# Turning the rows for the router with VectorE and a round trip through memory, in a cross-attention + mixture-of-experts kernel

## The chip, the cores and the metric

The kernel runs on one core of one Trainium2 chip. The metric is the device time of one execution in microseconds (us), lower is better; before the change the median of three runs is 1381.79 us (1377.54 to 1382.42).

## The reference, cut to what matters

8192 tokens (4 sequences of 2048) of width 512 go through two layers, all in float32:

```
x1  = layernorm(x)
q,k,v from x1 (512x512) and ctx (77 x 384); 16 heads of 32; softmax(q k / sqrt(32)) v
x2  = x + relu(attn @ W1 + b1) @ W2 + b2            # 512 -> 1024 -> 512
z   = layernorm(x2)
top1 = argmax(z @ Wg.T)                             # 8 experts, first of equal maxima
out = x2 + [gelu((layernorm(z)*s_e + b_e) @ w1_e + b1_e) @ w2_e + b2_e](top1)
```

Each token goes to one expert only. The router needs `x2` with its 512 features on the partitions (transposed), because TensorE contracts over partitions; the expert stage needs the normalised rows of `x2`, sorted by expert.

## The kernel before, in words

Tokens are worked in 16 blocks (`b` = 0 to 15) of 512, each in 4 subtiles (`SUB`) of 128 rows. Most products are done as three fp32r products of high and low parts (`split3`). One list, `sched`, written out by hand (lines 264 to 576), gives the order of all steps; `walk` then has every engine, SyncE (SP) and GpSimd (POOL) among them, issue its own part of each step in that order. Every engine's instructions run in the order of the list, so a wait in one step holds up all later steps of that engine. A bank of PSUM is chosen for each step that needs one: the one that was left longest ago.

One turn of the loop over `b` (line 364) is:

1. The last head group (`g` = 3) of the attention of block `b`: SUMS, RC (DVE reciprocal), AV, NORM, OUT. Between them TT: 16 PE transposes of the rows of `x2` of the previous block (`pe_tt`), evicted by ACT to `x2T` (TTOUT).
2. The up-projection: tiles `m` = 0 to 7 of 12 matmuls each (H on PE, two ACT passes HHI, one DVE pass HLO). The first two tiles are worked group by group (HK 0 to 3), as the attention output comes in; HK 3 is the last to become ready.
3. Woven into it: L (logits, 32 small matmuls), LT (transposed back), OH (one-hot of the maximum, DVE), RK (ranks, 8 small matmuls and six DVE operations), and SCAT (four indirect DMAs by POOL that scatter the normalised rows of block `b`-1 to `region`). When the scatters have landed, XLOAD (SP) loads the raw rows of block `b`+1 over them.
4. Also in it, on DVE: XSTAT for block `b`+1, a chain of 28 steps (statistics of `xn`, inverse root, normalising, four 32x32 block transposes into `xq`), dealt out by DRIP and finished by DRAIN at `m` = 4; and X2STAT, the chain that scales the rows of block `b`-1.
5. XTD: 16 DMAs by SP from `xq` back into `xn`, which complete the transposition of `x`; XTS then splits the result into `actA` (ACT high part, DVE low part).
6. The down-projection of subtiles 0 and 1 (YA, Y; 24 matmuls each), then Q of block `b`+1 (four tiles of 12 matmuls), which needs all four XTS. The maxima (SM), scores (ST, named by their matmul line 1126) and the rest of the attention of block `b`+1 follow, with the down-projection of subtiles 2 and 3 in pieces between them (YP).

`xn` is loaded by XNLOAD (SP). For `b` outside 3 to 10 (and under 15) the step stands in turn `b` behind HK 3 and loads block `b`+1; its lines are

```
            elif not PREP0 < b <= PREP0 + NE:
                step("XNLOAD", b + 1, 2)
                step("XNLOAD", b + 1, 0)
```

In turns 2 to 9 one expert's weights are also prepared. There the second weight is loaded by SP (E2_RAW, behind XLOAD in the list) into part of `xn`, split by ACT (E2_HIGH, between the ACT passes of Q tiles 1 and 2) and DVE (E2_LOW), and XNLOAD of block `b`+2 follows. In turns 3 to 10 DVE also scales the first weight (E1_ACC, in the up-projection).

`xq` lies in the low half of `actQ`, `x2T` in its high half. After the loop the experts run over 71 tiles of sorted rows.

Of the kernel before, what the change touches and what calls it, by code (L numbers as in the profile page):

```python
# [27 lines left out]
P = 128  # L28
D = 512
# [33 lines left out]
PREP0 = 2  # L63
DT = 2


def xattn_moe_kernel(nc, A, out):
    region = nc.dram_tensor("region", [NE * REG + P, ROW], F32).ap()
    v_parts = nc.dram_tensor("v_parts", [NB - 1, M, D], F32).ap()
    e1_parts = nc.dram_tensor("e1_parts", [P, KD, NE, EH], F32).ap()  # L70
    e2_parts = nc.dram_tensor("e2_parts", [2, P, NE, D], F32).ap()

# [161 lines left out]
    with ExitStack() as ctx:  # L234
        bank = [ctx.enter_context(nc.psum_tensor(f"bank{i}", [P, 512], F32)) for i in range(8)]

        def sem(name):
# [3 lines left out]
        L = {n: sem(f"ld_{n}") for n in (  # L241
            "bk", "first", "consts", "wk", "wv", "ctx", "wq", "w1", "w2", "e1", "e2", "eb", "jt", "tab", "pad0", "e1raw", "e2raw", "eb1")}
        ld_xn = [sem(f"ld_xn{s}") for s in range(SUB)]
        ld_x = [[sem(f"ld_x{i}_{s}") for s in range(SUB)] for i in range(2)]
        ld_xT = [sem(f"ld_xT{t}") for t in range(SUB)]
        st_v, ld_v = sem("st_v"), sem("ld_v")
# [7 lines left out]
            "dve_bks pe_k act_kf act_k dve_k pe_v dve_v pool_zero dve_const "  # L254
            "act_wq dve_wq act_w1 pool_w1 act_w2 dve_w2 act_kbd dve_sel dve_tri "
            "dve_xn dve_xnT pool_xb pe_xT act_xT dve_xT pe_q act_q dve_q pe_sm dve_max pe_mt act_mt pe_s act_exp "
            "pe_sums dve_rc pe_av dve_n act_o pool_o dve_o pe_h act_h dve_h pe_y dve_x2 dve_row pool_ones pe_gate dve_gate "
# [106 lines left out]
        for b in range(NBLK):  # L364
# [7 lines left out]
            if b:  # L372
                step("SUMS", b, g)
                step("RC", b, g)
                step("AV", b, g)
                for s in range(SUB - 1):
                    step("TT", b - 1, s)
                step("NORM", b, g)
                step("TTOUT", b - 1, 0)
# [27 lines left out]
            logits = 2  # L407
            ranks = 4 if last else 6
            for m in range(MF):
                if m >= 2:  # L410
                    step("H", b, m)
                step("HHI", b, m)
                if b and m == logits:
                    step("L", b - 1)
                    if last:
                        step("E2_LOAD", 0)
                if b and m == logits + 1:
                    step("LT", b - 1)
                if b and m == ranks:
# [10 lines left out]
                if b and m == logits + 1:  # L430
# [9 lines left out]
                if b and m == ranks:  # L440
                    for s in range(SUB):
                        step("SCAT", b - 1, s)
                    if not last:
                        step("XLOAD", b + 1)
# [32 lines left out]
            else:  # L477
# [85 lines left out]
        for t in range(-5, NT):  # L563
# [113 lines left out]
        def sp_setup(sp):  # L677

            sp.dma_start(bk[:], A["bk"]).then_inc(L["bk"], 16)
            sp.dma_start(ctxT[:], A["ctxT"]).then_inc(L["ctx"], 16)  # L680
            sp.dma_start(wk_raw[:], A["Wk"]).then_inc(L["wk"], 16)
# [102 lines left out]
        def sp_padload(sp):  # L784
            for s in range(SUB):
                sp.wait_ge(scat[0][s], 16 * (NBLK // 2))
            sp.dma_start(padrow[:], A["padrow"]).then_inc(L["tab"], 16)
            sp.dma_start(regions[:], A["regions"]).then_inc(L["tab"], 16)
            sp.wait_ge(L["tab"], 32)

            sp.dma_start(region[NE * REG:NE * REG + P, :], padrow[:]).then_inc(L["pad0"], 16)

# [32 lines left out]
        def dve_masks(dve):  # L825
            dve.wait_ge(L["consts"], 16 * NSMALL)
            dve.tensor_copy(tri[:], c_raw[:, 0:P])
            dve.tensor_copy(ones[:], c_raw[:, P:2 * P]).then_inc(S["dve_tri"], 1)

# [37 lines left out]
        def pe_kp(pe, m):  # L867
            p = own_bank(pe, "KP", m)
            if m == 0:
                pe.wait_ge(L["ctx"], 16)  # L870
                pe.wait_ge(L["wk"], 16)
            for k in range(KT):
# [99 lines left out]
        def dve_xstat(dve, b):  # L972

            def chain():
# [20 lines left out]
        def pe_xT(pe, b, s):  # L995
# [6 lines left out]
            mm.then_inc(S["pe_xT"], 1)  # L1002

        def sp_xtd(sp, b):

            sp.wait_ge(S["dve_xnT"], SUB * (b - DT + 1))
            for t in range(SUB):
                for f in range(HG):
                    sp.dma_start(xn[t][HD * f:HD * f + HD], xq[HD * t:HD * t + HD, f].rearrange("p k s j -> p (k s j)")
                                 ).then_inc(ld_xT[t], 16)  # L1010

# [192 lines left out]
        def pe_hk(pe, b, k):  # L1204

            if b == 0:
                pe.wait_ge(S["pool_w1"], 1)
# [4 lines left out]
            for m in range(2):  # L1212
                mm = h_products(pe, b, m, k)
# [69 lines left out]
        def dve_x2stat(dve, b):  # L1283


            def chain():
# [7 lines left out]
                for s in range(SUB):  # L1294
                    dve.wait_ge(S["pe_tt"], SUB * b + s + 1)
# [14 lines left out]
        def act_tt(act, b, s):  # L1310

            act.wait_ge(S["pe_tt"], SUB * b + s + 1)
            act.activation(x2T[b == NBLK - 1][:, :, P * s:P * s + P],
# [3 lines left out]
        def pe_l(pe, b):  # L1317

            p = own_bank(pe, "L", b)
            if b == 0:  # L1320
                pe.wait_ge(S["dve_const"], 1)
            pe.wait_ge(S["act_tt"], SUB * (b + 1))
            for k in range(KD):
                for s in range(SUB):
                    mm = pe.matmul(p[HD * s:HD * s + HD, 0:P], wg[:, k, :], x2T[b == NBLK - 1][:, k, P * s:P * s + P],  # L1325
                                   start=k == 0, stop=k == KD - 1)
# [274 lines left out]
        def sp_bload(sp, t):  # L1601
# [9 lines left out]
            if t == N1:  # L1611
                for s in range(SUB):
                    sp.wait_ge(scat[1][s], 16 * (NBLK // 2))
                sp.wait_ge(st_pad, 16 * NE)
                sp.wait_ge(L["pad0"], 16)
            if t >= NROW:
# [120 lines left out]
        def pool_store(pool, t):  # L1737
# [26 lines left out]
            "XT": {"pe": pe_xT, "act": act_xT, "dve": dve_xT},  # L1764
            "XTD": {"sp": sp_xtd},
            "XTS": {"act": act_xts, "dve": dve_xts},
# [21 lines left out]
            "Y": {"pe": pe_y, "dve": dve_y},  # L1788
            "X2STAT": {"dve": dve_x2stat},
            "TT": {"pe": pe_tt},  # L1790
            "TTOUT": {"act": act_tt},
# [125 lines left out]
```

## Time and profile before

| | |
|---|---|
| median of 3 runs | 1381.79 us |
| the profiled execution | 1382.66 us |
| its span | 1380.9 us |
| PE busy | 1358.1 us (98%) |
| DVE busy | 1000.4 us (72%) |
| ACT busy | 609.0 us (44%) |
| POOL busy | 338.0 us (24%) |
| mean granted TensorE clock | 0.999 |

The span is the stretch from the first to the last instruction in the trace; the execution's own time is 1.8 us longer. Busy time of PE is modelled from pipelined matmuls and so is no proof of work at the peak; the chain of waits says which engine the end is followed back to. An engine with 72% busy time may still be the one that is late in a short stretch.

### The profile page before, as it was taken

To read this page: it belongs to the slowest core of one execution; us is meant where nothing else is said; L and a number is where in the kernel's file an instruction comes from. 1 tells how busy PE (TensorE), PEld (TensorE's weight loads), DVE (VectorE), ACT (ScalarE), POOL (GpSimd) and SP (SyncE) were. 2 spreads that over 40 slices of the span, in tenths; PEclk is the share of its full clock that TensorE was granted. 3 is DMA by queue.
4 is the path that set the end of the run, shared out by engine and by line. 5 is a ranking of instruction groups with operands and counts; after the bars stand their busy time and mean duration, and the time that the engine had idled before them with its cause. 6 is when DMAs were issued, how large, how long until landed. Compare 5 with 4: busy or idle time off the path is not lost.

```text
span 1380.9 us, 23796 instructions
## 1 busy us (share of the span) xinstructions
PE 1358.1 (98%) x8366; PEld 1015.2 (74%) x8366; DVE 1000.4 (72%) x2129; ACT 609.0 (44%) x1146; POOL 338.0 (24%) x293
## 2 busy tenths in 40 slices
PE   7999999999999999999999999999999999999997
PEld 5486868677776768686868677776868686788996
DVE  6777677687778777777878677867676767558666
ACT  4434334443434343534344343524343433357885
POOL 2311211103020212121120202021212121128886
PEclk9999999999999999999999999999999999999999
DMA  7200302213040404131231303040303032559884
GB/s 297 76 29 3 93 31 67 88 36 123 22 139 9 138 24 117 50 101 61 63 99 31 123 25 114 6 122 1 117 7 106 18 92 76 189 170 302 285 260 140
DMA packets 66998, 132.85 MB, mean 96 GB/s; under 512 B 11241, under 2 KB 19698, under 8 KB 65986
## 3 DMA queue, kind: packets, MB, share of 16 engines
q1 hardware_dynamic: 56082, 97.63, 23.5%
q0 software_dynamic: 10800, 33.70, 6.4%
q8 instruction: 70, 1.15, 0.3%
q14 instruction: 46, 0.38, 0.1%
HBM read 73.77 MB, written 44.66 MB: 86 GB/s over the span
## 4 chain that ended last, share of the span: by engine, by line
PE 94%; DVE 2%; issue 1%; DMA 1%; POOL 1%; ACT 0%; another core or an unknown queue 0%; SPq 0%; POOLq 0%; ACTq 0%; DVEq 0%
PE bank L1221 25%; PE bank L1265 13%; PE bank L1245 12%; PE bank L1054 12%; PE bank L1144 8%; PE bank L1126 5%; PE bank L1647 4%; PE bank L1685 3%; PE bank L1079 2%; PE bank L1307 2%; PE bank L1631 2%; PE bank L1325 1%; PE bank L1098 1%; PE bank L898 1%; DMA region<-rows,pos 0%
## 5 line engine op out<-in xcount | busy, mean ns | idle before, releaser
L1221 PE MATMUL bank<-actA,w 128*128 128x512 f32 x1536 | 368.6, 395 | 1.4 <-DVE actA L1192 1.4
L1221 PEld LDWEIGHTS bank<-actA,w 128*128 128x128 f32 x1536 | 282.4, 188 | 63.4 <-issue 5.6
L1134 ACT ACTIVATE E<-bank 77x512 f32<-77x512 f32 x256 | 132.5, 592 | 172.8 <-PE bank L1126 172.7
L1265 PE MATMUL bank<-w,actH 128*128 128x512 f32 x768 | 195.7, 400 | 0.0
L1396 POOL DMA_INDIRECT region<-rows,pos x64 | 66.5, 1039 | 487.0 <-DVE rows L1296 451.6
L1054 PE MATMUL bank<-actA,wq 128*128 128x512 f32 x768 | 182.7, 390 | 0.0
L1245 PE MATMUL bank<-w,actH 128*128 128x512 f32 x768 | 179.6, 391 | 0.0
L1092 DVE TENSOR_REDUCE mx<-bank 128x4 f32<-128x308 f32 x256 | 104.8, 473 | 95.0 <-PE bank L1079 94.9
L1265 PEld LDWEIGHTS bank<-w,actH 128*128 128x128 f32 x768 | 138.7, 188 | 44.6 <-issue 18.3
L1245 PEld LDWEIGHTS bank<-w,actH 128*128 128x128 f32 x768 | 143.4, 188 | 29.5
L1054 PEld LDWEIGHTS bank<-actA,wq 128*128 128x128 f32 x768 | 142.7, 188 | 28.2 <-issue 0.5
L1230 ACT ACTIVATE actH<-bank,b 128x512 fp32r<-128x512 f32 x128 | 88.3, 690 | 159.3 <-PE bank L1221 157.7
L1235 DVE TENSOR_TENSOR actH<-bank,actH 128x512 fp32r<-128x512 f32 x128 | 87.6, 689 | 58.5 <-ACT bank L1231 56.5
L1161 DVE RECIPROCAL att<-bank 128x512 f32<-128x512 f32 x32 | 107.3, 3354 | 23.1 <-PE bank L1144 22.8
L1187 POOL TENSOR_TENSOR actA<-att,actA 128x512 fp32r<-128x512 f32 x32 | 41.0, 1281 | 331.7 <-ACT actA L1181 331.7
L1063 ACT ACTIVATE actQ<-bank,bq 128x512 fp32r<-128x512 f32 x64 | 43.9, 685 | 145.5 <-PE bank L1054 145.5
L1161 DVE RECIPROCAL csb<-bank 128x512 f32<-128x512 f32 x32 | 106.9, 3341 | 0.3 <-PE bank L1144 0.3
L1044 POOL TENSOR_TENSOR rows<-rows,b2bc 128x512 f32<-128x512 f32 x64 | 81.9, 1290 | 68.2 <-DMA rows<-in_x 43.3
L1231 ACT ACTIVATE bank<-bank,b 128x512 f32<-128x512 f32 x128 | 83.8, 655 | 0.0
L1275 DVE TENSOR_TENSOR rows<-bank,rows 128x512 f32<-128x512 f32 x64 | 44.2, 691 | 54.0 <-PE bank L1265 28.7
L1740 POOL DMA_INDIRECT out<-rowB x71 | 77.2, 1087 | 24.5 <-issue 11.8
L1647 PE MATMUL bank<-xhT,ew 128*128 128x128 f32 x568 | 75.9, 276 | 4.1 <-DVE gT L1674 2.3
(182 smaller groups left out, 1831.2 us busy)
## 6 DMA issues: line engine op xcount, KB each, us to landing
rowB<-region SPq DMA_DIRECT2D x71, 258.0 KB
xn<-in_x SPq DMA_DIRECT2D x64, 256.0 KB
rows<-in_x SPq DMA_DIRECT2D x64, 256.0 KB, 3.4
xn<-xq SPq DMA_DIRECT2D x224, 64.0 KB, 2.0
w_raw<-in_W SPq DMA_DIRECT2D x2, 2048.0 KB, 11.8
e_raw<-in_E SPq DMA_DIRECT2D x16, 256.0 KB, 3.4
region<-padrow SPq DMA_DIRECT2D x9, 258.0 KB, 2.3
e_parts<-e_high SPq DMA_DIRECT2D x8, 256.0 KB, 2.5
```

The source lines that it names most:

```text
L1054: mm = pe.matmul(p[:], w, a, start=k == 0 and j == 0, stop=k == KD - 1 and j == 2)
L1092: dve.tensor_reduce(to, p, AX, ALU.max, negate=True).then_inc(S["dve_max"], 1)
L1134: act.activation(E[0:M, g % 2, h, :], of("ST", b, g, h)[0:M, :], ACT.Exp).then_inc(S["act_exp"], 1)
L1144: mm = pe.matmul(p[r, :], held(h), E[0:M, g % 2, h, :], start=True, stop=True)
L1161: dve.reciprocal(att_of(g)[:], of("SUMS", b, g)[:]).then_inc(S["dve_rc"], 1)
L1221: mm = pe.matmul(p[:], w, a, start=k == 0 and j == 0, stop=k == KD - 1 and j == 2)
L1230: act.activation(actH[:, 0, m, :], p[:], ACT.Relu, bias=b1[:, m:m + 1])
L1231: act.activation(p[:], p[:], ACT.Relu, bias=b1[:, m:m + 1]).then_inc(S["act_h"], 1)
L1235: dve.tensor_tensor(actH[:, 1, m, :], of("H", b, m)[:], f32(actH[:, 0, m, :]), ALU.subtract).then_inc(S["dve_h"], 1)
L1245: mm = pe.matmul(p[:], a, w, start=m == 0 and j == 0, stop=m == MF - 1 and j == 2)
L1265: mm = pe.matmul(p[:], actH[:, ha, m, P * s:P * s + P], w2[:, hw, m, :], start=n == 0, stop=n == 23)
L1647: mm = pe.matmul(p, ew[t % 2][:, k, :], xhT[t % 2][:, k, :], start=k == 0, stop=k == KD - 1)
```

## The change

TT and TTOUT are left out for blocks 0 to 13 (`TP` = 14). In their place a step TTR turns the rows with four DVE block transposes into `xq`, one DMA stores `xq` to memory, SP waits for it to land, and four DMAs load it as `x2T`. XSTAT waits for the store before it writes `xq`. L, LT, OH, RK, SCAT and XLOAD move from the up-projection into the down-projection (in turns 1 to 14). Three tiles of the up-projection are worked by groups (`NHK` = 3). Four of the 16 DMAs of XTD go to POOL. DRIP deals nine steps in place of six.

```diff
+TP = NBLK - 2
+NHK = 3
+    x2_parts = nc.dram_tensor("x2_parts", [SUB, HD, HG, D], F32).ap()
@@ sched, turn b
                 step("AV", b, g)
-                for s in range(SUB - 1):
-                    step("TT", b - 1, s)
+                if last:
+                    for s in range(SUB - 1):
+                        step("TT", b - 1, s)
                 step("NORM", b, g)
...
                 step("OUT", b, g)
-                step("TTOUT", b - 1, 1)
-                step("TTOUT", b - 1, 2)
-            for m in range(2):
+                if last:
+                    step("TTOUT", b - 1, 1)
+                    step("TTOUT", b - 1, 2)
+                else:
+                    step("TTR", b - 1)
+            for m in range(NHK):
                 step("H", b, m)
             step("HK", b, 0)
             step("HK", b, 1)
             step("HK", b, 2)
-            if b:
+            if last:
                 step("TT", b - 1, SUB - 1)
                 step("TTOUT", b - 1, SUB - 1)
             step("HK", b, 3)
...
-                if b and m == logits:
+                if last and m == logits:
                     step("L", b - 1)
...
-                    step("DRIP", 6)
+                    step("DRIP", 6 if last or b == 0 else 9)
...
                 step("YA", b, 0)
-                for s in range(SUB):
-                    step("XB", b + 1, s)
+                if b:
+                    step("L", b - 1)
                 step("Y", b, 0)
+                if b:
+                    step("LT", b - 1)
+                    step("OH", b - 1)
                 for s in range(2):
                     step("XTS" if b + 1 >= DT else "XT", b + 1, s)
                 step("YA", b, 1)
+                if b:
+                    step("RK", b - 1)
+                    for s in range(SUB):
+                        step("SCAT", b - 1, s)
+                    step("XLOAD", b + 1)
+                for s in range(SUB):
+                    step("XB", b + 1, s)
@@ dve_xstat
                 if b >= DT:
-                    dve.wait_ge(S["pe_s"], KD * b)
+                    dve.wait_ge(st_x2, 16 * (b - 1))
@@ sp_xtd; pool_xtd issues the other four
+        NSP = 12
+                    if HG * t + f < NSP:
+                        sp.dma_start(*quarter(t, f)).then_inc(ld_xT[t], 16)
@@ new
+        def dve_ttr(dve, b):
+            dve.wait_ge(S["pe_s"], KD * (b + 2))
+            dve.wait_ge(S["dve_x2"], SUB * (b + 1))
+            for s in range(SUB):
+                dve.transpose(xq[:, :, :, s, :], rows[b % 2][:, s, 0:D].rearrange("p (k f j) -> p f k j", k=KD, j=HD)
+                              ).then_inc(S["dve_tq"], 1)
+
+        def sp_ttr(sp, b):
+            sp.wait_ge(S["dve_tq"], SUB * (b + 1))
+            if b:
+                sp.wait_ge(ld_x2T, 16 * SUB * b)
+            sp.dma_start(x2_parts.rearrange("t i f n -> (t i) (f n)"), xq[:].rearrange("p f k s j -> p (f k s j)")
+                         ).then_inc(st_x2, 16)
+            sp.wait_ge(st_x2, 16 * (b + 1))
+            sp.wait_ge(S["pe_s"], KD * (b + 2))
+            for t in range(SUB):
+                sp.dma_start(x2T[0][:, t, :], x2_parts[t].rearrange("i f n -> f i n")).then_inc(ld_x2T, 16)
@@ pe_l
-            pe.wait_ge(S["act_tt"], SUB * (b + 1))
+            if b < TP:
+                pe.wait_ge(ld_x2T, 16 * SUB * (b + 1))
+                x = x2T[0][:].rearrange("p t (k s j) -> p k s t j", k=KD, s=SUB)
```

The rest of the diff gathers a few semaphores of the set-up and adapts the waits to the new counts.

## Rows read from the trace of the kernel before

**Rows 1.** The page: busy time by engine; the chain's shares by engine.
```profile
PE 1358.1 (98%) x8366; PEld 1015.2 (74%) x8366; DVE 1000.4 (72%) x2129; ACT 609.0 (44%) x1146; POOL 338.0 (24%) x293
PE 94%; DVE 2%; issue 1%; DMA 1%; POOL 1%; ACT 0%; another core or an unknown queue 0%; SPq 0%; POOLq 0%; ACTq 0%; DVEq 0%
```
**Rows 2.** The chain of waits in turn 14: start us, us, what.
```profile
1097.58 1.46 PE bank L1307 x12
1099.04 4.13 PE bank L1221 x18
1103.18 0.44 PE bank L1307 x4
...
1107.75 1.01 PE bank L1325 x32
...
1133.93 5.44 PE bank L1054 x24
...
1148.12 1.09 PE bank L1126 x16
```
**Rows 3.** VectorE in order of time, turn 14: start us, us, instruction, idle before.
```profile
1102.60 2.46 DVE L977 BATCH_NORM_STATS2 bn<-xn 128x6 f32<-128x512 f32 x4
...
1105.62 0.69 DVE L1235 TENSOR_TENSOR actH<-bank,actH 128x512 fp32r<-128x512 f32 x1
...
1115.45 1.30 DVE L990 STREAM_TRANSPOSE xq<-xn 128x512 f32<-128x512 f32 x2
...
1125.69 1.67 DVE L1296 TENSOR_SCALAR rows<-rows,r 128x512 f32<-128x512 f32 x4
```
**Rows 4.** Busy time by stretch: PE, PEld, DVE, ACT, POOL, then PEclk, DMA share, GB/s.
```profile
1102.60:1133.90 31.30, 31.30 (x175) 25.43 (x174) 23.28 (x77) 13.40 (x23) 4.18 (x4) 1.00 0.24 67
1375.00:1381.00 6.00, 0.27 (x2) 0.00 (x0) 1.01 (x2) 0.00 (x0) 3.13 (x3) 0.81 0.03 0
```
**Rows 5.** SyncE in order of time, turns 13 and 14: start us, us, DMA issues.
```profile
1063.24 2.45 SPq L718 DMA_DIRECT2D xn<-in_x  x4
1118.16 10.56 SPq L1009 DMA_DIRECT2D xn<-xq  x16
```
**Rows 6.** DMA issues: KB each, median us from issue to landing.
```profile
rows<-in_x SPq DMA_DIRECT2D x64, 256.0 KB, 3.4
e_parts<-e_high SPq DMA_DIRECT2D x8, 256.0 KB, 2.5
e<-e_parts SPq DMA_DIRECT2D x1, 2048.0 KB, 8.4
```
**Rows 7.** GpSimd in order of time: first scatters of turns 2, 4 and 9.
```profile
234.78 0.99 POOL L1396 DMA_INDIRECT region<-rows,pos  x1 [30.99 <-DVE rows L1296]
...
385.36 0.99 POOL L1396 DMA_INDIRECT region<-rows,pos  x1 [33.24 <-DVE rows L1296]
...
758.49 0.99 POOL L1396 DMA_INDIRECT region<-rows,pos  x1 [33.21 <-DVE rows L1296]
```
**Rows 8.** SyncE in order of time, turn 9.
```profile
769.04 0.62 SPq L748 DMA_DIRECT2D e_raw<-in_E  x1
```
**Rows 9.** ScalarE in order of time: E2_HIGH in turns 2, 4 and 9.
```profile
247.65 0.64 ACT L1437 ACTIVATE e_high<-e_raw 128x512 fp32r<-128x512 f32 x1 [0.93 <-DMA e_raw<-in_E]
...
398.76 0.63 ACT L1437 ACTIVATE e_high<-e_raw 128x512 fp32r<-128x512 f32 x1 [3.15 <-DMA e_raw<-in_E]
...
774.07 0.63 ACT L1437 ACTIVATE e_high<-e_raw 128x512 fp32r<-128x512 f32 x1 [5.33 <-DMA e_raw<-in_E]
```
**Rows 10.** The chain of waits, turn 9: its start, Q, ACT's pass, first scores.
```profile
725.73 1.46 PE bank L1307 x12
...
762.57 5.44 PE bank L1054 x24
...
774.62 0.67 ACT actQ L1063
...
777.83 1.16 PE bank L1126 x14
```

More of the change, by code:

```diff
@@ L241, in xattn_moe_kernel @@
         L = {n: sem(f"ld_{n}") for n in (
-            "bk", "first", "consts", "wk", "wv", "ctx", "wq", "w1", "w2", "e1", "e2", "eb", "jt", "tab", "pad0", "e1raw", "e2raw", "eb1")}
+            "bk", "first", "consts", "wk", "wv", "wq", "w1", "w2", "e1", "e2", "eb", "jt", "tab", "e1raw", "e2raw", "eb1")}
         ld_xn = [sem(f"ld_xn{s}") for s in range(SUB)]
         ld_x = [[sem(f"ld_x{i}_{s}") for s in range(SUB)] for i in range(2)]
+        st_x2, ld_x2T = sem("st_x2"), sem("ld_x2T")
         ld_xT = [sem(f"ld_xT{t}") for t in range(SUB)]
@@ L375, in xattn_moe_kernel @@
                 step("AV", b, g)
-                for s in range(SUB - 1):
-                    step("TT", b - 1, s)
+                if last:
+                    for s in range(SUB - 1):
+                        step("TT", b - 1, s)
                 step("NORM", b, g)
-                step("TTOUT", b - 1, 0)
+                if last:
+                    step("TTOUT", b - 1, 0)
                 step("OUT", b, g)
-                step("TTOUT", b - 1, 1)
-                step("TTOUT", b - 1, 2)
-            for m in range(2):
+                if last:
[4 more added lines that the diff above has]
+            for m in range(NHK):
                 step("H", b, m)
@@ L387, in xattn_moe_kernel @@
             step("HK", b, 2)
-            if b:
+            if last:
                 step("TT", b - 1, SUB - 1)
@@ L407, in xattn_moe_kernel @@
             logits = 2
-            ranks = 4 if last else 6
+            ranks = 4
             for m in range(MF):
-                if m >= 2:
+                if m >= NHK:
                     step("H", b, m)
                 step("HHI", b, m)
-                if b and m == logits:
+                if last and m == logits:
                     step("L", b - 1)
-                    if last:
-                        step("E2_LOAD", 0)
-                if b and m == logits + 1:
+                    step("E2_LOAD", 0)
+                if last and m == logits + 1:
                     step("LT", b - 1)
-                if b and m == ranks:
+                if last and m == ranks:
                     step("RK", b - 1)
@@ L426, in xattn_moe_kernel @@
                 if m:
-                    step("DRIP", 6)
+                    step("DRIP", 6 if last or b == 0 else 9)
                 if context is not None and m == 0:
                     step("VLOAD", context)
-                if b and m == logits + 1:
+                if last and m == logits + 1:
                     step("OH", b - 1)
@@ L439, in xattn_moe_kernel @@
                     step("X2STAT", b - 1)
-                if b and m == ranks:
+                if last and m == ranks:
                     for s in range(SUB):
                         step("SCAT", b - 1, s)
-                    if not last:
-                        step("XLOAD", b + 1)
                 if last and m == 5:
@@ L789, in sp_padload @@
             sp.wait_ge(L["tab"], 32)
[L791 removed]
+            sp.dma_start(region[NE * REG:NE * REG + P, :], padrow[:]).then_inc(st_pad, 16)
         def pool_setup(pool):
@@ L827, in dve_masks @@
             dve.tensor_copy(tri[:], c_raw[:, 0:P])
-            dve.tensor_copy(ones[:], c_raw[:, P:2 * P]).then_inc(S["dve_tri"], 1)
+            dve.tensor_copy(ones[:], c_raw[:, P:2 * P])
         def act_kcopy(act, i):
@@ L869, in pe_kp @@
             if m == 0:
-                pe.wait_ge(L["ctx"], 16)
-                pe.wait_ge(L["wk"], 16)
+                pe.wait_ge(L["wk"], 32)
             for k in range(KT):
@@ L1002, in pe_xT, with quarter @@
             mm.then_inc(S["pe_xT"], 1)
+        NSP = 12
+        def quarter(t, f):
+            return xn[t][HD * f:HD * f + HD], xq[HD * t:HD * t + HD, f].rearrange("p k s j -> p (k s j)")
         def sp_xtd(sp, b):
@@ L1008, in sp_xtd, with pool_xtd @@
                 for f in range(HG):
-                    sp.dma_start(xn[t][HD * f:HD * f + HD], xq[HD * t:HD * t + HD, f].rearrange("p k s j -> p (k s j)")
-                                 ).then_inc(ld_xT[t], 16)
+                    if HG * t + f < NSP:
+                        sp.dma_start(*quarter(t, f)).then_inc(ld_xT[t], 16)
+        def pool_xtd(pool, b):
+            pool.wait_ge(S["dve_xnT"], SUB * (b - DT + 1))
+            for t in reversed(range(SUB)):
+                for f in range(HG):
+                    if HG * t + f >= NSP:
+                        nc.gpsimd.dma_start(*quarter(t, f)).then_inc(ld_xT[t], 16)
         def act_xts(act, b, t):
@@ L1195, in pe_h @@
             own_bank(pe, "H", b, m)
-            if m < 2:
+            if m < NHK:
                 return
@@ L1206, in pe_hk @@
             if b == 0:
-                pe.wait_ge(S["pool_w1"], 1)
+                pe.wait_ge(S["pool_w1"], (NHK + 1) // 2)
             if k < KD - 1:
@@ L1211, in pe_hk @@
                 pe.wait_ge(S["dve_o"], b + 1)
-            for m in range(2):
+            for m in range(NHK):
                 mm = h_products(pe, b, m, k)
@@ L1294, in chain @@
                 for s in range(SUB):
-                    dve.wait_ge(S["pe_tt"], SUB * b + s + 1)
+                    if b < TP:
+                        dve.wait_ge(S["dve_tq"], SUB * b + s + 1)
+                    else:
+                        dve.wait_ge(S["pe_tt"], SUB * (b - TP) + s + 1)
                     dve.tensor_scalar(r[:, s, 0:D], r[:, s, 0:D], r1[:, s:s + 1], None, ALU.mult
@@ L1310, in act_tt @@
         def act_tt(act, b, s):
-            act.wait_ge(S["pe_tt"], SUB * b + s + 1)
+            act.wait_ge(S["pe_tt"], SUB * (b - TP) + s + 1)
             act.activation(x2T[b == NBLK - 1][:, :, P * s:P * s + P],
@@ L1321, in pe_l @@
                 pe.wait_ge(S["dve_const"], 1)
-            pe.wait_ge(S["act_tt"], SUB * (b + 1))
+            if b < TP:
+                pe.wait_ge(ld_x2T, 16 * SUB * (b + 1))
+                x = x2T[0][:].rearrange("p t (k s j) -> p k s t j", k=KD, s=SUB)
+            else:
+                pe.wait_ge(S["act_tt"], SUB * (b - TP + 1))
+                x = x2T[b == NBLK - 1][:].rearrange("p k (s t j) -> p k s t j", s=SUB, j=HD)
             for k in range(KD):
                 for s in range(SUB):
-                    mm = pe.matmul(p[HD * s:HD * s + HD, 0:P], wg[:, k, :], x2T[b == NBLK - 1][:, k, P * s:P * s + P],
+                    mm = pe.matmul(p[HD * s:HD * s + HD, 0:P], wg[:, k, :], x[:, k, s],
                                    start=k == 0, stop=k == KD - 1)
@@ L1613, in sp_bload @@
                     sp.wait_ge(scat[1][s], 16 * (NBLK // 2))
-                sp.wait_ge(st_pad, 16 * NE)
-                sp.wait_ge(L["pad0"], 16)
+                sp.wait_ge(st_pad, 16 * (NE + 1))
             if t >= NROW:
@@ L1764, in xattn_moe_kernel @@
             "XT": {"pe": pe_xT, "act": act_xT, "dve": dve_xT},
-            "XTD": {"sp": sp_xtd},
+            "XTD": {"sp": sp_xtd, "pool": pool_xtd},
             "XTS": {"act": act_xts, "dve": dve_xts},
@@ L1789, in xattn_moe_kernel @@
             "X2STAT": {"dve": dve_x2stat},
+            "TTR": {"sp": sp_ttr, "dve": dve_ttr},
             "TT": {"pe": pe_tt},
```

8 lines of the change are left out of this document (4 added, 4 removed).

## The prediction

> **What bounds the kernel now.** I read the page first: PE is busy 98% of the span and 94% of the chain that ended last is PE's [rows 1]. DVE at 72% is second, so the question is where in a turn it has no slack. The chain of one ordinary turn (14) shows what PE does there [rows 2]. I count time in a turn from the moment at which AV of the last head group is done on PE; in turn 14 that is 1097.58, where the transposes (line 1307) begin. They take 1.46 + 0.44 = 1.90 us, the logits (line 1325) 1.01 us, and Q of the next block (line 1054) starts at 1133.93 - 1097.58 = 36.35. Without the transposes the same PE work puts Q at 34.4. The first scores (line 1126) follow Q's start by 1148.12 - 1133.93 = 14.2 us.
>
> Next I read DVE in the same turn [rows 3]. It ends the attention's last pass at 5.0 and starts the statistics of `xn` at 1102.60 at once: the data is there, because SP had issued those loads at 1063.24, a turn earlier [rows 5]. From 5.0 to Q DVE is busy 23.28 of 31.3 us [rows 4]: 8 us of slack, in pieces, with PE never idle. (The transpose of `x` and the scaling of the rows, 1.30 us for two and 1.67 us for four, are among it [rows 3].)
>
> In turns with expert preparation I look at the queue behind the scatters. Turn 9 begins at 725.73 [rows 10]; the first scatter starts at 758.49, which is 32.8 [rows 7]. SP's reload of the rows waits for each scatter to land, E2_RAW is issued behind it at 769.04 [rows 8], and ACT, whose next pass is E2_HIGH, sits idle 5.33 us until it lands, at 774.07; only then comes the pass for Q tile 2, at 774.62 [rows 9, 10]. From the first scatter to E2_HIGH is 15.6 us here and 13.4 us in turn 4 [rows 7, 9]; these are the longest and the shortest of turns 3 to 9, and the mean of the seven is 14.5. Turn 9 already pays: its first scores come 15.3 us after Q [rows 10], not 14.2.
>
> **The change, part by part.**
>
> *Transposes on PE.* Removed in 14 turns: 14 x 1.90 = 26.6 us [rows 2], all of it on the chain. L, LT and RK move but stay on PE; they cost what they cost. ACT loses four evictions a turn, which are under cover and count nothing. With the transposes gone HK 3 would be reached at 4.1, ahead of DVE's last pass at 5.0; the third tile by groups brings it to 27 x 0.229 = 6.2 (18 matmuls took 4.13 us [rows 2]), so it costs and saves nothing.
>
> *TTR on DVE.* Four block transposes, 1.30 us for two that overlap [rows 3], so 2.5 us: DVE is free at 7.55 and not at 5.0. In a turn where `xn` is already loaded the 8 us of slack take that.
>
> *The round trip on SP.* One store of 1 MB, then a wait in SP's own queue for its landing. No row has 1 MB; 256 KB stores land in 2.5 us and a 2 MB read in 8.4 us [rows 6], which are my two ends; between them by size lies 5.0, and I take 4.8. The store lands at 7.55 + 0.1 + 4.8 = 12.45. Four loads follow; like those of `xn` they take rows in four groups, so I price their issue at 2.45 / 4 = 0.62 us each [rows 5]. The last lands at 12.45 + 3 x 0.62 + 3.4 = 17.7. The logits want it at 24.6, behind YA: nothing lost.
>
> *What is queued behind that wait.* In turns 1, 2 and 11 to 14 XNLOAD of block `b`+1 stands in SP's list behind HK 3, and so now behind TTR. Before, SP ran ahead and the loads were issued in the turn before; now they can't be issued until the store has landed. The tile that DVE wants first (`s` = 0) is the seventh DMA of the eight: issued at 12.45 + 6 x 0.62 = 16.15, landed 3.4 us later [rows 6], 19.6. Its bounds: 16.3 with the 2.5 us store and a landing of 2.4 (the shortest of the loads of `rows`), 24.8 with 8.4 and the 5.0 us that E2_RAW took in turn 9 behind 1 MB of other loads. DVE has issued its wait for that tile right behind TTR, ahead of HLO of tile 0, so everything of DVE stands still from 7.55 to 19.6.
>
> From there DVE is the bound up to Q. Its list, each from turn 14's rows or their like: statistics 2.5 and 0.5, eight HLO at 0.6 = 4.8, inverse roots 2 x 2.4, normalising 1.8, transposes 2.5, aggregates and small copies of X2STAT 0.5, scaling of rows 1.7, LT and OH 1.2, RK 0.85, Y with its statistics 1.3, four XTS 2.5: together 25.0, against 23.28 of busy time in the same stretch, whose dependent small steps leave gaps [rows 3, 4]. The last XTS ends at 44.6 and Q starts there, 8.3 us later than before. PE starts YA with the first freed bank and then waits for HLO, tile by tile.
>
> Five turns (1, 11, 12, 13, 14) lose 8.3 each: 41.5 us. Turn 2 also has E2_RAW. Its RK ends at 43.35, and its scatter to E2_HIGH took 12.9 us before [rows 7, 9], so E2_HIGH is at 56.2. The pass for Q tile 2 ends 1.2 us after E2_HIGH starts and the first scores come 2.55 us later (774.07, 775.29, 777.83) [rows 9, 10]: 60.0 against 50.6, 9.4 us lost.
>
> *Ranks and scatters later, turns 3 to 9.* Here `xn` is loaded in time. DVE runs TTR, XSTAT, E1_ACC, HLO 7 to 24.2, then X2STAT (4.6 us) to 28.8, Y 1.3, LT 0.2, OH 1.1 to 31.4, two XTS to 32.65, RK to 33.5. PE's YA 1 ends at 31.2, so it hardly waits. XTS end at 34.8, Q starts at 34.9, where it was 36.84 [rows 10]. But the first scatter now waits for RK and not for the scaled rows: 33.65 against 32.8. Everything behind it on SP keeps its distance, so E2_HIGH comes at 33.65 + 14.5 and the scores at 33.65 + 14.5 + 1.2 + 2.55 = 51.9. Q's own pace would put them at 49.1. Taken turn by turn (before: the later of 51.05 and scatter + 3.75; after: the same with the scatter 0.9 later) the seven turns change by 0.4, -0.25, 0.5, 0.9, 0.6, 0.9, 0.9: 4.0 us lost in all. PE's 1.9 us become waiting at SM and the scores. Ends: -2.2 us a turn if E2_RAW is never late, +1.7 if DVE's backlog puts RK a microsecond later.
>
> *Turn 10* has neither late load nor E2: -1.7 us.
>
> *POOL's share of XTD.* SP's 16 issues took 10.56 us [rows 5], 12 take 7.9. XTS of the last subtile waits less, but DVE is there later still: nothing. Its four DMAs on POOL (1 us each, as for a scatter [rows 7]) are done before the scatters.
>
> **Sum.** 41.5 + 9.4 + 4.0 - 1.7 = +53.2 us. The profiled execution took 1382.66 us (span 1380.9 and 1.8 around it), 0.9 above the median of the runs, so 1435.9: I say 1436.
>
> The Trainium skill, "DMA: Bandwidth & Descriptors", section "Anatomy of one DMA", gives a fixed 2.0 us and bytes over 436 GB/s, estimated 4.4 us for the store, and the sum would be 2 us lower by it. The trace's 2.5 us for 256 KB agrees with it; its 8.4 us for 2 MB is above its 6.8.
>
> **The rivals.**
>
> *E2_RAW is in time.* Were the chain behind the scatters shorter (SP's reload waits less because the scatters land when DMA is quiet), turns 3 to 9 would keep their gain, -2.2 each in place of +4.0 in all, and turn 2 would lose 8.3: 1436 - 20.5 = 1415. For it: the distance varies from 13.4 to 15.6. Against: it would have to shrink by nearly 3 us in every turn.
>
> *The clock falls.* PE now has pauses of 3 us and more in 13 turns. The granted clock is 1.00 all through the blocks and 0.81 in the last 6 us, where PE worked 0.27 us [rows 4]. If each pause costs one tile of 12 matmuls (2.73 us) at 1.2 GHz in place of 2.4, that is 2.7 us each: 16 us in the six late turns, 35 us in all 13: 1452 to 1471. Against: the late turns' pauses are broken by matmuls. The Trainium skill, "TensorE: Matmul & The Clock Gate", section "What's actually happening", says that an idle PE is set back to half rate; no row here has such a pause inside the blocks.
>
> *The round trip is late for L.* If `x2T` lands after 24.6, 7 us later than I price it, PE waits in all turns. At 3 us past that point the eight turns without a late `xn` lose 24 us: 1460. For it only that 2 MB are in flight at once.
>
> *Not slower: DVE's slack takes the wait.* One place decides, the landing of `xn` tile 0. Q comes 25.0 after it, so at a landing of 11.35 the late turns lose nothing, and from about 9 they keep the 1.9 us. If SP's wait cost little and the scatters too were in time, the full 26.6 us would come: 1356. For it: 8 us of DVE slack. Against: store, six issues and a landing would have to fit into 3.8 us, and my lowest bounds give 8.7.
>
> **How the numbers follow.** Forecast 0.62, its own range 1420 to 1455; E2 in time 0.13; clock 0.14; round trip late 0.05; not slower 0.06. The landing's bounds alone move six turns by -3.3 to +5.2 us each: 1416 to 1467. The range 1413 to 1463 holds the forecast, the first rival and the smaller form of the second. What a measurement can tell from no change is about 0.5% (7 us). Faster only in the last rival: 0.04; within it 0.02; slower 0.94.
>
> **What would show it.** In the profile after: a wait of DVE's line for `bn` from `xn` on the load from `in_x`, about 12 us in each of six turns, 70 us in sum; the loads of `xn` issued some 12 us into those turns; turns of about 82 us there, 74 to 76 in turns 3 to 9 and 72.7 in turn 10; PE idle before lines 1245 and the up-projection's heirs with DVE's `actH` as releaser; ACT waiting some 7 us a turn for `e_raw`. If those turns are as short as turn 10, the step about SP's queue is wrong and with it the sign.

## The result and the profile after

The changed kernel takes 1534.06 us (median of 4, 1533.02 to 1545.4) against 1382.11: a ratio of 1.113, 95% interval 1.108 to 1.118. It is 152 us slower. The profiled execution, from which the rows of the kernel after are read, took 1545.4 us, 11 us above the median. The forecast was 1436 us, range 1413 to 1463: the sign and the place were right, the size was wrong by a factor of nearly three.

First the page of the kernel after, to lay beside [rows 1]: busy time, the chain by engine, and the new DMA issues.

```profile
PE 1380.7 (89%) x8142; PEld 1015.4 (66%) x8142; DVE 1035.5 (67%) x2185; ACT 582.4 (38%) x1090; POOL 367.6 (24%) x349
PEclk9999697999999999999999999799796997999999
PE 60%; DMA 15%; DVE 12%; issue 6%; SPq 4%; POOL 2%; ACT 1%; POOLq 0%; ACTq 0%; DVEq 0%
x_parts<-xq SPq DMA_DIRECT2D x14, 1024.0 KB, 3.8
```

PE (TensorE) issues 224 matmuls fewer and its share of the chain falls from 94% to 60%; DMA has 15% of it. The granted clock, 9 in every slice before, has dips. The store of 1 MB lands in 3.8 us, where I had 4.8.

Next who waited for whom (total us, times, longest), all engines and then PE:

```profile
DVE bn L992 <- DMA xn<-in_x: 163.4, 13, 24.7
ACT e_high L1494 <- DMA e_raw<-in_E: 53.9, 8, 8.8
PE bank L1272 <- DVE actH L1262: 111.6, 15, 15.8
PE bank L1382 <- DMA x2T<-x_parts: 17.9, 8, 4.1
PE bank L1106 <- issue: 13.9, 8, 3.8
```

The first row is the wait that the forecast named, DVE's statistics on the loads of `xn`, but with 163 us in place of 70. The third is what it does to PE: the down-projection (line 1272) stands until DVE has made `actH`. The fourth is the rival about a late round trip: the logits wait for `x2T` in eight turns. The fifth is PE's wait at the maxima in turns 2 to 9, where ACT's wait in the second row (E2_HIGH, 6.7 us a turn; about 7 were forecast) is the cause.

Turn 1 from PE's side (AV ends at 129.0, where the up-projection begins), from SP's, with the third load of `xn` again by itself, and from DVE's, to its last XTS and beyond (start us, us):

```profile
129.03 22.10 PE L1248 MATMUL bank<-actA,w 128*128 128x512 f32 x96
```
```profile
136.63 0.33 SPq L1347 DMA_DIRECT2D x_parts<-xq  x1
140.49 2.44 SPq L1352 DMA_DIRECT2D x2T<-x_parts  x4
142.97 9.58 SPq L734 DMA_DIRECT2D xn<-in_x  x4
...
147.62 2.44 SPq L734 DMA_DIRECT2D xn<-in_x  x1
```
```profile
134.12 2.48 DVE L1339 STREAM_TRANSPOSE xq<-rows 128x512 f32<-128x512 f32 x4
161.11 0.69 DVE L992 BATCH_NORM_STATS2 bn<-xn 128x6 f32<-128x512 f32 x1 [24.51 <-DMA xn<-in_x]
163.68 1.88 DVE L992 BATCH_NORM_STATS2 bn<-xn 128x6 f32<-128x512 f32 x3 [1.87 <-DMA xn<-in_x]
...
185.97 1.29 DVE L1049 TENSOR_TENSOR actA<-xn,actA 128x512 fp32r<-128x512 f32 x2
187.50 0.69 DVE L1302 TENSOR_TENSOR rows<-bank,rows 128x512 f32<-128x512 f32 x1 [0.24 <-PE bank L1272]
```

SP issues the loads of `x2T` and `xn` as forecast, behind the store. But DVE gets its first tile 24.5 us after TTR, not 12: at 32.1 in the turn, not 19.6. The seventh load, which brings that tile, is issued at 147.62, 18.6 in the turn where I had 16.15, and its data is there 13.5 us later where I had 3.4. From there to the last XTS is 26.2 us, of which 1.9 are a second wait: 24.3 of work, where I had 25.0. Busy time by stretch says why the data was so late; the last two columns are the share of the 16 DMA engines and GB/s:

```profile
141.00:161.00 20.00, 10.12 (x45) 8.07 (x43) 0.00 (x0) 5.47 (x9) 0.00 (x0) 0.86 0.25 95
161.00:166.00 5.00, 0.00 (x0) 0.00 (x0) 2.98 (x9) 0.00 (x0) 0.00 (x0) 0.50 0.10 40
428.00:433.00 5.00, 5.00 (x43) 3.83 (x33) 1.54 (x4) 2.44 (x5) 0.00 (x0) 0.66 0.10 30
```

For 20 us, while DVE and soon PE starve, DMA moves 95 GB/s at a share of 0.25, which is what four busy engines of sixteen give. The trace of before had it to be read, in the same loads of `xn`, hidden a turn ahead:

```profile
1071.00:1073.00 2.00, 2.00 (x14) 1.79 (x13) 0.55 (x2) 0.52 (x2) 0.00 (x0) 1.00 0.26 102
```

The second and third rows above show the clock (column PEclk): 0.50 after PE has stood still, that is 1.2 GHz of 2.4; and 0.66 over the stretch of turn 4 in which PE works behind the pause at the logits:

```profile
427.72 1.26 PE L1382 MATMUL bank<-x2T,wg 128*32 128x128 f32 x32 [1.97 <-DMA x2T<-x_parts]
428.91 4.40 PE L1272 MATMUL bank<-w,actH 128*128 128x512 f32 x12
433.15 0.27 PE L1396 MATMUL bank<-ident,csb 128*128 128x128 f32 x1
433.17 2.98 PE L1272 MATMUL bank<-w,actH 128*128 128x512 f32 x12
```

The first 12 matmuls of Y take 4.40 us, the next 12, at full clock, 2.98. The Trainium skill, "TensorE: Matmul & The Clock Gate", section "What's actually happening", has an idle PE set back to half rate; the trace agrees, with 0.50.

Turn by turn, from the first matmul of the up-projection to the next turn's, in us, for the kernels of this study. The times in brackets are medians, the turns those of one profiled execution each (turn 14 holds the transposes of block 14 and is 1.3 us longer where the others have none):

| kernel (time, us) | 1 | 2 | 3 to 9, mean | 10 | 11 to 14, mean |
|---|---|---|---|---|---|
| before (1382 to 1386) | 73.9 | 73.9 | 74.7 | 74.4 | 74.0 |
| after (1534.1) | 96.1 | 97.4 | 79.5 | 74.3 | 96.6 |
| loads_16_engines (1488.3) | 89.9 | 91.4 | 76.4 | 72.7 | 90.3 |
| all_loads_late_order (1459.9) | 85.2 | 87.9 | 76.4 | 72.7 | 85.6 |
| xn_before_ttr (1427.7) | 76.8 | 79.5 | 80.0 | 77.5 | 75.1 |
| loads_and_order (1385.2) | 72.5 | 74.6 | 76.8 | 72.7 | 72.9 |
| fixed_e2_first (1356.9) | 72.5 | 72.5 | 72.7 | 72.7 | 72.9 |
| moves_only (1410.3) | 74.3 | 74.4 | 78.9 | 74.4 | 74.3 |
| moves_e2_first (1382.1) | 74.2 | 74.3 | 74.5 | 74.4 | 74.3 |
| before_e2_first (1381.0) | 73.9 | 73.9 | 74.5 | 74.4 | 74.0 |

The loss sits where the forecast put it: turns 1, 2 and 11 to 14, +22 to +23 us each where 8.3 and 9.4 were forecast (136 us of the profiled execution's 162), and turns 3 to 9, +4.8 each where 0.6 was.

### The profile page after: what moved, and what is told of

Its sections match the earlier page's. It is cut to its first block, busy times and chain, and to the rows that moved or that the text cites. A ratio compares the mean times of both kernels' runs of the same rounds, so it can differ in the third digit from the quotient of the medians.

```text
span 1543.3 us, 23415 instructions
## 1 busy us (share of the span) xinstructions
PE 1380.7 (89%) x8142; PEld 1015.4 (66%) x8142; DVE 1035.5 (67%) x2185; ACT 582.4 (38%) x1090; POOL 367.6 (24%) x349
## 3 DMA queue, kind: packets, MB, share of 16 engines
q1 hardware_dynamic: 62802, 123.31, 24.8%
## 4 chain that ended last, share of the span: by engine, by line
PE 60%; DMA 15%; DVE 12%; issue 6%; SPq 4%; POOL 2%; ACT 1%; POOLq 0%; ACTq 0%; DVEq 0%
PE bank L1292 12%; PE bank L1248 9%; PE bank L1081 8%; PE bank L1272 7%; PE bank L1171 6%; DMA xn<-in_x 5%; PE bank L1153 5%; PE bank L1703 4%; DMA x2T<-x_parts 3%; PE bank L1741 3%; DMA x_parts<-xq 3%; SPq L734 3%; DVE csb L1188 2%; PE bank L1106 2%; PE bank L1687 2%
## 5 line engine op out<-in xcount | busy, mean ns | idle before, releaser
L1248 PE MATMUL bank<-actA,w 128*128 128x512 f32 x1536 | 354.9, 391 | 0.0
L1248 PEld LDWEIGHTS bank<-actA,w 128*128 128x128 f32 x1536 | 286.7, 188 | 72.2 <-issue 12.8
L1272 PE MATMUL bank<-w,actH 128*128 128x512 f32 x768 | 216.4, 436 | 111.6 <-DVE actH L1262 111.6
L1272 PEld LDWEIGHTS bank<-w,actH 128*128 128x128 f32 x768 | 154.8, 210 | 159.6 <-DVE actH L1262 123.5
L1292 PE MATMUL bank<-w,actH 128*128 128x512 f32 x768 | 198.5, 404 | 0.0
L1292 PEld LDWEIGHTS bank<-w,actH 128*128 128x128 f32 x768 | 140.6, 190 | 45.5 <-issue 18.9
L992 DVE BATCH_NORM_STATS2 bn<-xn 128x6 f32<-128x512 f32 x64 | 40.0, 678 | 163.4 <-DMA xn<-in_x 163.4
L1037 POOL DMA_DIRECT2D xn<-xq x56 | 29.2, 536 | 438.3 <-DVE xq L1005 438.3
L1262 DVE TENSOR_TENSOR actH<-bank,actH 128x512 fp32r<-128x512 f32 x128 | 83.9, 674 | 14.7 <-ACT bank L1258 14.6
L1095 DVE SCALAR_TENSOR_TENSOR actQ<-bank,bq,actQ 128x512 fp32r<-128x512 f32 x64 | 47.7, 746 | 56.6 <-ACT actQ L1090 56.6
## 6 DMA issues: line engine op xcount, KB each, us to landing
x_parts<-xq SPq DMA_DIRECT2D x14, 1024.0 KB, 3.8
```

Source lines behind the costliest of these rows:

```text
L1248: mm = pe.matmul(p[:], w, a, start=k == 0 and j == 0, stop=k == KD - 1 and j == 2)
L1262: dve.tensor_tensor(actH[:, 1, m, :], of("H", b, m)[:], f32(actH[:, 0, m, :]), ALU.subtract).then_inc(S["dve_h"], 1)
L1272: mm = pe.matmul(p[:], a, w, start=m == 0 and j == 0, stop=m == MF - 1 and j == 2)
L1292: mm = pe.matmul(p[:], actH[:, ha, m, P * s:P * s + P], w2[:, hw, m, :], start=n == 0, stop=n == 23)
```

## The experiments

### The loads of x2T on sixteen engines

The Trainium skill, "DMA: Bandwidth & Descriptors", section "Why a DMA increments its semaphore by 16 and not by 1", says that a DMA is spread over the largest number of engines, at most 16, that divides the outermost dimension of both sides. The loads of `x2T` and the permuted ones of `xn` have 4 there. The prediction did not apply it.

```diff
-            for t in range(SUB):
-                sp.dma_start(x2T[0][:, t, :], x2_parts[t].rearrange("i f n -> f i n")).then_inc(ld_x2T, 16)
+            for f in range(HG):
+                sp.dma_start(x2T[0][HD * f:HD * f + HD], x2_parts[:, :, f, :].rearrange("t i n -> i t n")
+                             ).then_inc(ld_x2T, 16)
```

> The changed kernel with one thing altered: the four loads of x2T each take one feature group (32 partitions, all four subtiles) and not one subtile in four row groups; same bytes, same number of DMAs. Theory A (a DMA whose outer dimension is 4 runs on 4 of the 16 DMA engines, as the DMA share of 0.25 and 102 GB/s after the store in the trace say): x2T lands some 4 us after its first issue and not 13 to 15, the xn tile that DVE waits for lands some 6 us earlier in the six late turns (three xn loads on 4 engines remain), and PE no longer pauses at the logits in turns 3 to 10: 6 x 6 + 8 x 4 = about 66 us less than 1534, 1468 us. Rival B (the 2 MB are slow because they are 2 MB in 2 KB pieces): no change, 1530 to 1538.

1488.3 us (ratio to before 1.074, 1.070 to 1.078), 46 us less than the changed kernel, where 66 were expected. The rival that nothing changes falls. While the loads of `x2T` run, the DMA share in turn 1 is now 0.52, so more than four engines are at work:

```profile
141.00:145.00 4.00, 4.00 (x19) 3.30 (x19) 0.00 (x0) 2.26 (x4) 0.00 (x0) 1.00 0.52 141
```

The logits of turn 4 no longer wait, and keep their clock:

```profile
410.59 1.08 PE L1383 MATMUL bank<-x2T,wg 128*32 128x128 f32 x32
411.60 3.02 PE L1272 MATMUL bank<-w,actH 128*128 128x512 f32 x12
```

The six late turns fell by about 6 us each, as expected. Turns 3 to 9 fell by 3.1 on average, less than the 4 expected: what remains there is the wait at E2_HIGH.

### The loads of xn too, still behind TTR

```diff
-                    x = x.rearrange("(t s j) d -> s t j d", s=SUB, j=HD)[s]
+                    if s == s0:
+                        x = x.rearrange("(t s j) d -> t j s d", s=SUB, j=HD)
+                        for t in range(SUB):
+                            sp.dma_start(xn_all[HD * t:HD * t + HD, s0:s0 + 2, :], x[t][:, s0:s0 + 2]
+                                         ).then_inc(ld_xn[s0], 16)
+                    continue
...
-                    dve.wait_ge(ld_xn[s], 16 * (b + 1))
+                    if b < DT:
+                        dve.wait_ge(ld_xn[s], 16 * (b + 1))
+                    else:
+                        dve.wait_ge(ld_xn[s - s % 2], 16 * DT + 16 * SUB * (b - DT + 1))
```

The loads of `x2T` are those of the run above. The edit alters more than the number of engines: `xn` now comes in eight DMAs of 128 KB and not in four of 256 KB, and DVE waits for the last of the eight and not for the third of the four.

> loads_16_engines with the xn loads too taken by 32 rows each, still behind TTR in SP's list: the kernel as the prediction priced it, with the wait but with loads at full speed. Theory A (my step on SP's wait was right and only the landing was mis-sized): DVE resumes some 13 us after it ends TTR, the six late turns fall from 90 to about 82.5 us, 45 us less than loads_16_engines: about 1443 us. Rival B (the landing is not set by the number of DMA engines): the six turns stay at 88 to 90 us, over 1475.

1459.9 us (1.056, 1.053 to 1.059): 28 us less again, not 45; between the two expectations, with the late turns at 85.0 to 87.9 where A had 82.5 and B 88 or more. SP and DVE in turn 1, the DMA share meanwhile, and the time from issue to landing (median us) in that stretch:

```profile
140.60 1.76 SPq L1360 DMA_DIRECT2D x2T<-x_parts  x4
142.41 3.72 SPq L734 DMA_DIRECT2D xn<-in_x  x8
```
```profile
152.20 2.47 DVE L1000 BATCH_NORM_STATS2 bn<-xn 128x6 f32<-128x512 f32 x4 [15.47 <-DMA xn<-in_x]
```
```profile
145.00:150.00 5.00, 5.00 (x24) 4.14 (x23) 0.00 (x0) 2.47 (x4) 0.00 (x0) 1.00 1.07 231
```
```profile
xn<-in_x SPq DMA_DIRECT2D x8, 128.0 KB, 6.1
```

The landing is 15.5 us after TTR, against 24.5 in the changed kernel and 18.3 with only `x2T` fast. In the changed kernel the last of the 2 MB was there 23.2 us after the first issue (140.49 to 163.68), here after 11.6 us, at up to 231 GB/s in place of 95. So the number of engines did set most of the delay. Where I had 7.1 us for the first tile of `xn` (six issues, 3.7, and one landing, 3.4), these 11.6 are twelve issues, 5.5, and a landing of 6.1 behind all the other data. This run is close to the change as the prediction priced it, four issues apart, and it is 24 us above the predicted 1436.

### The loads of xn ahead of TTR

```diff
+            if b and not last and not PREP0 < b <= PREP0 + NE:
+                step("XNLOAD", b + 1, 2)
+                step("XNLOAD", b + 1, 0)
             if b:
                 step("SUMS", b, g)
...
-            elif not PREP0 < b <= PREP0 + NE:
+            elif b == 0:
                 step("XNLOAD", b + 1, 2)
                 step("XNLOAD", b + 1, 0)
```

> The changed kernel with XNLOAD placed ahead of the attention's last group, so ahead of TTR in SP's list, in turns 1, 2 and 11 to 14; the x2T loads stay as they are. Theory A (SP's wait for the store holds back the xn loads): DVE's wait for xn goes (163 us to under 10), the six turns fall from 96 to about 76 us, as turn 4's pause at the logits now shows in them too: about 120 us less, 1414 us. Rival B (DVE has no room for the four new transposes whatever the order): the six turns stay above 85 us and the time above 1465.

1427.7 us (1.030, 1.021 to 1.039), 106 us less. DVE's wait for `xn` is 4.8 us, once, at the start:

```profile
DVE bn L995: 4.8, 1
```

The six turns are 74.5 to 79.5 us, so DVE has room for its four transposes, and rival B falls. It is 14 us above the number I gave. Now the logits wait for `x2T` in all fourteen turns:

```profile
PE bank L1385 <- DMA x2T<-x_parts: 36.0, 14, 4.0
```

### Both

> Both alterations together. Theory A: PE keeps its 1.9 us in turns 1, 2 and 10 to 14 (about 72 us each), and turns 3 to 9 stay up to 1 us above the kernel before, because the scatters wait for the ranks and E2_RAW for the scatters: about 1371 us, range 1365 to 1380. Rival B (the later logits and ranks cost more than the transposes gave): over 1388. Rival C (E2_RAW is not late once DMA traffic is lighter): 1357.

The kernel has the edits of `loads_16_engines` and `xn_before_ttr`.

1385.2 us, ratio 0.999 (0.997 to 1.001): no difference from before. Turns 1 and 10 to 13 are 72.5 to 72.7, as expected, so the transposes' gain is there. Turns 3 to 9 take it all back, 76.8 against at most 75.7 expected, so the time is 14 us over the 1371 I gave, outside its range of 1365 to 1380, and only just short of rival B's 1388. Turn 4 on POOL, SP, ACT and PE, and last the same matmuls of YP and of the scores in turn 4 of the kernel before:

```profile
388.23 1.20 POOL L1457 DMA_INDIRECT region<-rows,pos  x1 [12.11 <-DVE pos L1451]
```
```profile
399.63 0.62 SPq L767 DMA_DIRECT2D e_raw<-in_E  x1
```
```profile
404.32 0.63 ACT L1498 ACTIVATE e_high<-e_raw 128x512 fp32r<-128x512 f32 x1 [8.41 <-DMA e_raw<-in_E]
```
```profile
405.62 0.80 PE L1109 MATMUL bank<-kbd,actQ 128*128 128x308 f32 x4 [3.42 <-issue]
406.26 1.95 PE L1295 MATMUL bank<-w,actH 128*128 128x512 f32 x5
408.14 1.57 PE L1156 MATMUL bank<-actQ,k_hl 32*78 32x512 f32 x12
```
```profile
402.32 1.32 PE L1265 MATMUL bank<-w,actH 128*128 128x512 f32 x5
403.57 0.93 PE L1126 MATMUL bank<-actQ,k_hl 32*78 32x512 f32 x12
```

The turn began at 354.55 and its first scatter at 388.23, 33.7 in the turn, where I had 33.65. But E2_HIGH follows it by 16.1 us in this turn and by 15.4 on average over turns 3 to 9, where the mean before was 14.5. And PE, having stood 3.4 us, works on at half clock: the five matmuls of YP take 1.95 us where the same five took 1.32 before, the twelve of the scores 1.57 where they took 0.93.

### Only the moves

The PE transposes stay, there is no TTR; the later logits, ranks, scatters and reloads remain, the third tile by groups, and the rest.

```diff
-TP = NBLK - 2
+TP = 0
...
-                if last:
-                    for s in range(SUB - 1):
-                        step("TT", b - 1, s)
+                for s in range(SUB - 1):
+                    step("TT", b - 1, s)
...
-                else:
-                    step("TTR", b - 1)
...
-                    dve.wait_ge(st_x2, 16 * (b - 1))
+                    dve.wait_ge(S["pe_s"], KD * b)
```

> The changed kernel with the PE transposes and their ACT evictions put back for all blocks, no TTR, no round trip; what is left of the change is the later logits, ranks, scatters and reloads, the third tile by groups, DRIP 9 and POOL's share of XTD. Theory A: the first scatter of turns 3 to 9 comes some 2.5 us later than in the kernel before and E2_HIGH with it, so these seven turns grow by 2 us each and the rest stays: about 1396 us. Rival B (the moves are free): 1378 to 1386.

1410.3 us (1.018, 1.013 to 1.023), 14 us above what A said. Turns 3 to 9 grow by 4.2 us each, the others by 0.4 at most. So rival B falls, and the moves alone make the kernel slower, by 24 us against the kernel before. That is about what the transposes give, in line with `loads_and_order`, which only came out even.

### E2_RAW ahead of the reload

XLOAD waits in SP's queue for each scatter to land; E2_RAW stands behind it and needs none of that.

```diff
-                    step("XLOAD", b + 1)
                 for s in range(SUB):
                     step("XB", b + 1, s)
...
                     step("E2_RAW", prep)
                     step("XNLOAD", b + 2, 2)
+                if b:
+                    step("XLOAD", b + 1)
```

With the moves only:

> moves_only with the same move of XLOAD. Theory A (all of the 24 us that the moved logits, ranks and scatters cost came through E2_RAW behind the scatters): 1410 down to 1386 within 3 us, turns 3 to 9 at 74.8 us. Rival B (the moves cost by themselves): above 1395.

1382.1 us (0.998, 0.997 to 0.999), 28 us less than moves_only; turns 3 to 9 at 74.5. All of the moves' cost came through that queue. In loads_and_order:

> loads_and_order with XLOAD moved behind E2_RAW and the first two xn loads in SP's list, so that SP no longer waits for the scatters before it asks for the expert's weight. Theory A (turns 2 to 9 are long only because E2_HIGH waits for a weight whose load stands behind the reload of rows: 74.6 and 75.5 to 78.3 us a turn): these turns fall to 72.6 and 73.0 us, 28.7 us in sum, 1385 to about 1357 us, ratio 0.98. Rival B (the pause at the third Q tile comes from the later ranks on DVE, or the reload of rows becomes late in its turn): 1370 or more.

1356.9 us (five runs, 1356.58 to 1358.66), ratio 0.980 (0.979 to 0.982). This version is faster than both kernels. ACT's wait is nearly gone and so is PE's pause; POOL's first sum of the reloaded rows comes later, at 396.67, and nothing waits for it:

```profile
388.87 0.63 ACT L1499 ACTIVATE e_high<-e_raw 128x512 fp32r<-128x512 f32 x1 [0.98 <-DMA e_raw<-in_E]
390.50 0.69 ACT L1094 ACTIVATE actQ<-bank,bq 128x512 fp32r<-128x512 f32 x1 [0.99 <-PE bank L1085]
```
```profile
PE 1335.6 (99%) x8142; PEld 991.8 (73%) x8142; DVE 1032.4 (76%) x2185; ACT 576.3 (43%) x1090; POOL 365.9 (27%) x349
PE 96%; issue 1%; DVE 1%; DMA 0%; POOL 0%; POOLq 0%; SPq 0%; ACT 0%; DVEq 0%
```

The same with the loads of `xn` on sixteen engines:

> The same with the xn loads also taken by 32 rows each, so on all 16 DMA engines. Theory A: they are issued a turn ahead and hide whatever they take, so no difference from fixed_e2_first, within 2 us. Rival: their quarter-speed transfer delays the other loads that queue behind them on the same four engines (e_raw among them), so 3 us or more faster.

1357.2 us, no difference (0.981, 0.979 to 0.982): a load issued a turn ahead may be slow.

And the kernel before with the move of XLOAD alone:

> The kernel before with only XLOAD moved behind E2_RAW and the two xn loads. It is the fair rival of fixed_e2_first: what of the gain is the order of SP's list and what the transposes. Theory A: turns 6, 8 and 9 lose 0.6, 0.2 and 1.1 us of delay, 1.9 us in all, ratio 0.9986; the other turns had just enough slack.

1381.0 us, ratio 0.9975 (0.9964 to 0.9986): turns 6, 8 and 9 lost their extra 0.6, 0.2 and 1.2 us, 2.0 in all. The medians are 3.9 us apart; the rest is in no turn of the profiled executions. The ratio 0.980 of the fixed version is then almost all the transposes': between moves_e2_first and fixed_e2_first lie 25.3 us, 14 turns of 1.8, where the prediction counted 14 times 1.90. Against the kernel before with XLOAD moved, the fixed version is 24 us faster.

## Why the prediction missed, step by step

- *Transposes on PE, 26.6 us.* Right: 25.3 us once nothing else was late.
- *TTR on DVE is under cover where `xn` is there.* Right: with the order mended, turns 1 and 11 to 13 are 72.5 us.
- *The store of 1 MB, 4.8 us.* Near: 3.8 us. The 4.4 us that the prediction estimated beside it from the Trainium skill, "DMA: Bandwidth & Descriptors", section "Anatomy of one DMA", comes from a fit for DMAs that GpSimd issues; this store is SP's. That no row has 1 MB was not so: the trace of before has one load of that size (`wq_raw<-in_Wq SPq DMA_DIRECT2D x1, 1024.0 KB, 7.3`), 7.3 us among the other loads of the set-up. It would have made the term worse.
- *The last of the four loads of `x2T` lands at 17.7, 7 us before the logits want it.* Wrong, and the rival that I gave 0.05 happened: in turn 4 the logits could start only 26.8 in the turn, 9 us after my 17.7, and the eight turns wait 17.9 us in sum, with half clock behind it.
- *XNLOAD is held back behind SP's wait, DVE stands, 25.0 us of DVE work follow.* The mechanism was right: moving the loads takes 106 us away. The work was 24.3 us.
- *The tile lands 3.4 us after its issue, 19.6 in the turn.* This is the term that failed. It measured 32.1, outside my bounds of 16.3 to 24.8: the issue came 2.4 us later than priced, since SP took 2.4 us for one load of `xn` and not 0.62, and the landing took 13.5 us and not 3.4. I took the landing from loads of `rows`, which have 128 plain rows, and not from loads with the shape in question, which have four row groups and keep a quarter of the engines busy (share 0.25). For the issue time I had told the two shapes apart; for the landing not. The bounds were drawn from rows of another shape and so bounded nothing. With `x2T` and `xn` on sixteen engines the landing was at 23.0 and the time 1459.9: that takes away 74 of the 98 us that I was off.
- *The rest, 24 us.* In that run turns 1, 2 and 11 to 14 are some 3.5 us longer than priced, since a landing behind 2 MB of loads took 6.1 us and not 3.4, and since that kernel has four issues more (together 11.6 us where I had 7.1); how much is due to each was not taken apart. And turns 3 to 9 are 1 us longer than priced.
- *Turns 3 to 9 lose 0.6 us each.* The chain (ranks, scatter, reload, E2_RAW, E2_HIGH) was right. In the changed kernel these turns are 4.8 us longer and not 0.6, and it is the chain's start that was late: the logits begin 27.2 in the turn on average, 2.4 us after the 24.7 of the runs in which they do not wait, and in turns 4, 5, 6, 8 and 9 the clock falls behind that wait. So the first scatter comes at 35.1 and 35.2 in turns 3 and 7 and at 37.3 to 39.3 in the others, and not at 33.65. From there to E2_HIGH it is 14.6 us on average, as priced. With `x2T` in time (loads_and_order) the first scatter is at 33.7, as priced, and two other sizes are off: the distance from scatter to E2_HIGH, 15.4 us on average, and the half clock behind a pause of some 3 us, which I had kept apart as a rival at 0.14.
- *Turn 10 gains 1.7 us.* In the changed kernel it gained 0.1 (74.3 against 74.4), as its logits wait for `x2T` too. With `x2T` on sixteen engines it took 72.7 us, as forecast.
- *The clock.* It fell, in both kinds of turn. In the late turns it seems to have cost nothing, as DVE set the pace (its work there took 24.3 us, less than I priced with PE at full clock); no run tested that. In turns 3 to 9 it did cost: 1.3 us in the one place shown in turn 4 of loads_and_order (0.63 in YP, 0.64 in the scores), 1.4 us at the logits of turn 4 after the change (4.40 against 2.98).

The outcomes on the slow side were not alternatives. The late `xn`, the late `x2T` and the clock all came together, the first two from loads that keep a quarter of the engines busy and the third behind the pauses that they made, and my range treated them as if only one could be true.

What stays open: why the distance from scatter to E2_HIGH grew by 0.9 us on average from the kernel before to loads_and_order. About half of it is a later issue of E2_RAW (10.6 us behind the first scatter and not 10.2), the other half a longer landing (4.7 us and not 4.3); no run took it apart. How long PE must stand for its clock to fall was not measured either.

## What to carry to other kernels

Before you hide or unhide a DMA, read its landing from DMAs of the same access pattern: look at the DMA share while it runs alone, and if it is 0.25, it keeps only a quarter of the engines busy. Here 2 MB took 23.2 us in that shape and 11.6 us spread over all. A blocking wait in SyncE's program is a wait for every load that stands behind it; list them all, and put those first that depend on nothing in the wait. Where PE is the bound in every turn, as here, check each transfer that was timed against PE's pace: the saving came in full only when these were moved earlier too.

## What the runs showed of the hardware

- DMAs whose outermost dimension is 4 ran at 95 to 102 GB/s and a DMA share of 0.25 to 0.26. With 32 outermost the share rose to 0.52 and above, at 141 to 231 GB/s, and the logits' data came early enough in every turn. The Trainium skill's rule on the spread of a DMA, named above, agrees.
- SP's issues themselves stretched while such DMAs were in flight, to 9.58 us for four loads of `xn`, where they took 2.45 us a turn ahead [rows 5] and 3.04 us once `x2T` ran on sixteen engines.
- TensorE's granted clock was 0.50 (1.2 GHz) after pauses of 2 to 16 us, and 512-column matmuls that follow each other took 0.37 us each in place of 0.25 (4.40 us for twelve, then 2.98).
